# Rotary products in an attention kernel: the cosine product taken out of PSUM by VectorE, the sine product and the sum on GpSimd, and the second key and query projections ahead of the second value product

## The reference

```python
q = proj(Wq, bq) * scale            # 16 heads x 128, scale = 128 ** -0.5
k = proj(Wk, bk)
v = proj(Wv, bv)
q = t * cos(pos) + rotate_half(t) * sin(pos)     # the same for k
sim = einsum('bhid,bhjd->bhij', q, k)            # causal
out = softmax(sim) @ v
return out @ Wo + bo
```

## Time and profile before

| what | value |
|---|---|
| median of 3 runs | 1030.65 us (1030.63 to 1032.5) |
| the profiled execution's own time | 1031.39 us |
| its span, first to last instruction | 1029.6 us |
| PE busy | 970.8 us, 94% |
| DVE busy | 784.1 us, 76% |
| POOL busy | 764.7 us, 74% |
| ACT busy | 669.5 us, 65% |
| mean granted clock of TensorE | 0.996 of full |

### The profile page before, as it was taken

How to read it: one execution, slowest core, us unless ns; L and a number is a source line. 1 busy time by engine, 2 the same in 40 slices (tenths; PEclk the granted TensorE clock), 3 DMA queues, 4 the chain that set the end, 5 groups by cost and what they waited for, 6 DMA issues and landing times.

```text
span 1029.6 us, 19698 instructions
## 1 busy us (share of the span) xinstructions
PE 970.8 (94%) x5853; PEld 854.3 (83%) x5853; DVE 784.1 (76%) x1605; ACT 669.5 (65%) x1385; POOL 764.7 (74%) x532
## 2 busy tenths in 40 slices
PE   6988999999999999999999999999999999998897
PEld 5877888888888888888888888888888788887787
...
GB/s 248 166 79 139 118 118 101 107 131 114 102 101 139 127 113 111 138 127 100 115 97 141 103 111 97 148 127 107 107 142 124 109 99 159 139 103 42 1 42 42
DMA packets 86597, 116.74 MB, mean 113 GB/s; under 512 B 10468, under 2 KB 61732, under 8 KB 86564
## 3 DMA queue, kind: packets, MB, share of 16 engines
...
...
## 4 chain that ended last, share of the span: by engine, by line
PE 62%; POOL 11%; issue 7%; DMA 7%; ACT 6%; DVE 4%; SPq 2%; ACTq 0%; POOLq 0%; DVEq 0%
PE ps_r L1504 13%; PE ps_r L1503 13%; PE ps_r L1502 13%; PE ps_s L1502 5%; PE ps_s L1504 4%; PE ps_s L1503 4%; PE ps_t L1663 4%; POOL swapped L734 3%; DMA swapped<-straight 3%; POOL qk_lo L744 3%; POOL straight L735 2%; DMA side_out<-squares 2%; DMA side_p<-side_out 2%; ACT straight L885 2%; ACT probs L1014 1%
## 5 line engine op out<-in xcount | busy, mean ns | idle before, releaser
L734 POOL TENSOR_TENSOR swapped<-swapped,sin_sb 128x512 f32<-128x512 f32 x124 | 167.5, 1351 | 135.5 <-DMA swapped<-straight 135.0
L1014 ACT ACTIVATE probs<-ps_s,neg_max 128x128 f32<-128x128 f32 (+7 forms) x256 | 190.2, 743 | 109.3 <-DVE neg_max L1394 109.3
L1394 DVE CUSTOM_DVE_ANT_0 ps_s<-ps_s,mask_wide 128x128 f32<-128x128 f32 (+7 forms) x256 | 193.4, 755 | 31.1 <-PE ps_s L1504 29.4
L744 POOL TENSOR_TENSOR qk_lo<-straight,qk_hi 128x512 fp32r<-128x512 f32 x124 | 161.8, 1315 | 63.3 <-ACT qk_hi L898 63.2
L1314 DVE TENSOR_TENSOR pT_lo<-ps_t,pT_hi 128x512 fp32r<-128x512 f32 (+3 forms) x260 | 126.7, 498 | 75.7 <-ACT pT_hi L992 75.6
L735 POOL TENSOR_TENSOR straight<-straight,cos_sb 128x512 f32<-128x512 f32 x124 | 181.8, 1466 | 0.0
L1235 DVE TENSOR_TENSOR straight<-straight,swapped 128x512 f32<-128x512 f32 x126 | 147.1, 1168 | 15.2 <-POOL straight L735 14.7
L754 POOL TENSOR_TENSOR pT_lo<-side_p,pT_hi 128x1024 fp32r<-128x1024 f32 (+1 forms) x62 | 150.9, 2434 | 0.0
L1502 PE MATMUL ps_s<-qk_hi 128*128 128x512 f32 (+4 forms) x384 | 139.8, 364 | 9.7 <-POOL qk_lo L744 9.5
L992 ACT ACTIVATE pT_hi<-ps_t 128x512 fp32r<-128x512 f32 (+3 forms) x260 | 117.1, 450 | 43.0 <-PE ps_t L1663 41.3
L1353 DVE SCALAR_TENSOR_TENSOR y<-ps_r,inv_sum,y 128x256 f32<-128x256 f32 x248 | 108.4, 479 | 35.7 <-PE ps_r L1504 31.7
...
## 6 DMA issues: line engine op xcount, KB each, us to landing
...
side_p<-side_out SPq DMA_DIRECT2D x124, 128.0 KB, 3.0
...
side_p<-side_out SPq DMA_DIRECT2D x124, 112.0 KB, 2.5
...
```

The lines of the kernel that those rows point to most:

```text
L734: pool.tensor_tensor(swapped[:, q, :], swapped[:, q, :], sin_sb[:, cs], ALU.mult)
L744: pool.tensor_tensor(lo, rope_buffers(piece)[0][:, RANK[piece] % 2, :], hi.bitcast(F32), ALU.subtract)\
L1014: nc.scalar.activation(halved(t, probs[:, P_AT[step] * P:(P_AT[step] + t + 1) * P]), score_rows(step, t), ACT.Exp, bias=neg_max[:, t:t + 1 ...
L1394: nc.vector.tensor_tensor_reduce(rows, rows, halved(t, mask_wide[:, SEQ - n_keys:SEQ]), -1.0, -MASKED, ALU.add, ALU.min, accum_out=neg_max ...
```

## The change

The cosine product no longer waits for the swap. VectorE reads the projection in PSUM, adds the bias and multiplies by the cosines in one instruction (`qk_cosine`, line 1267 of the new file), into `qk_cos`, which lies where `qk_lo` of that piece will lie. GpSimd multiplies `swapped` by the sines and adds `qk_cos` to it in place. ScalarE and GpSimd then split `swapped`, not `straight`. Since the instruction has room for one scale only, the query weights are scaled as they are split (`w_high`), and the low part of the query weights moves from GpSimd to VectorE (`wq_low`, once ahead of the first units and once in a pass). TensorE's bank is now free when `cos_ready` says so. SyncE's swap now waits until the low part of the piece two before has been taken.

The plans of all engines are rewritten. On TensorE K1 goes ahead of `scores:3`, Q1 ahead of `scores:4`, and P1 behind `scores:4`.

```diff
-TENSOR_PLAN make:K0+ make:Q0+ scores:0 turn:6.0- turn:7.0- scores:1 scores:2 turn:7.1- make:P0- turn:0.0
-        make:P1- scores:3 make:W00- make:K1+ scores:4 make:W01- turn:2.0 make:Q1+
-        make:W10- scores:5 make:W11- make:V0 turn:4.0 scores:6 make:V1 turn:5.0 scores:7
-        turn:5.1
+TENSOR_PLAN make:K0+ make:Q0+ scores:0 turn:6.0- turn:7.0- scores:1 scores:2 turn:7.1- make:P0- turn:0.0
+        make:K1+ scores:3 make:Q1+ scores:4 make:P1- make:W00- turn:2.0 scores:5 make:W01- make:W10- turn:4.0
+        scores:6 make:W11- make:V0 turn:5.0 scores:7 make:V1 turn:5.1
...
-SYNC_PLAN = """swap:K0+ swap:Q0+ side:1 back:1 swap:K1+ swap:Q1+ side:3 back:3"""
+SYNC_PLAN = """swap:K0+ swap:Q0+ side:1 swap:K1+ swap:Q1+ back:1 side:3 back:3"""
...
                 sp.wait_ge(straight_ready, ps.rank(piece, 1))
+                if RANK[piece] >= 6:
+                    sp.nop(nofuse=True)
+                    sp.wait_ge(qk_ready, ps.rank(piece, -1))
...
-                pool.tensor_tensor(swapped[:, q, :], swapped[:, q, :], sin_sb[:, cs], ALU.mult)
-                pool.tensor_tensor(straight[:, q, :], straight[:, q, :], cos_sb[:, cs], ALU.mult).then_inc(rotated, 1)
+                pool.tensor_tensor(swapped[:, q, :], swapped[:, q, :], sin_sb[:, at_], ALU.mult).then_inc(rotated, 1)
+                pool.wait_ge(cos_ready, ps.cosines(piece))
+                pool.wait_ge(rotated, ps.rank(piece, 1))
+                pool.tensor_tensor(swapped[:, q, :], swapped[:, q, :], qk_cos[:, unit % 2, which, at_], ALU.add).then_inc(qk_sum, 1)
...
-                nc.scalar.activation(hi, raw, ACT.Copy).then_inc(w_hi_ready[j], 1)
+                nc.scalar.activation(hi, raw, ACT.Copy, scale=SCALE if j == WQ else 1.0).then_inc(w_hi_ready[j], 1)
...
+            def wq_low(n):
+                raw, hi, lo = w_buffers[WQ]
+                dve.wait_ge(w_hi_ready[WQ], n + 1)
+                nc.vector.scalar_tensor_tensor(lo, raw, SCALE, hi.bitcast(F32), ALU.mult, ALU.subtract).then_inc(w_ready[WQ], 1)
...
+            def qk_cosine(ps, piece):
+                dve.wait_ge(straight_ready, ps.rank(piece, 1))
+                nc.vector.scalar_tensor_tensor(qk_cos[:, unit % 2, which, at_], ps_r[:, ps.bank(piece), :], bias, cos_sb[:, at_],
+                                               ALU.add, ALU.mult).then_inc(cos_ready, 1)
...
                 if old[0] == "qk":
-                    pe.wait_ge(straight_ready, ps.rank(old, 1))
+                    if old in FIRST_QK:
+                        pe.wait_ge(straight_ready, ps.rank(old, 1))
+                    else:
+                        pe.wait_ge(cos_ready, ps.cosines(old))
```

More of the change, by code:

```diff
@@ L124 @@
     SCALAR_PLAN: """exp:0 out:K0+ xout:4 xout:5 exp:1 out:Q0+ xout:6 xout:7 exp:2 turn:0.0 exp:3 high:K0+ high:Q0+
-        side:1 exp:4 out:K1+ turn:2.0 out:Q1+ exp:5 turn:4.0 high:V0 high:V1 high:K1+ turn:5.0 exp:6 split:O side:3 turn:5.1 high:Q1+""",
-    VECTOR_PLAN: """max:0 max:1 xlow:4 xlow:5 max:2 side:1 max:3 add:K0+ xlow:6 xlow:7 turn:0.0 sum:B0 add:Q0+ sum:B1
-        max:4 gates:0 turn:2.0 side:3 max:5
-        turn:4.0 max:6 low:V0 add:K1+ low:V1 max:7 turn:5.0 add:Q1+ turn:5.1""",
@@ L129 @@
-    POOL_PLAN: """rotate:K0+ rotate:Q0+ low:K0+ low:Q0+ rotate:K1+ rotate:Q1+ low:K1+ side:1 low:Q1+ side:3 bias:0 split:O"""}
+        exp:4 out:K1+ turn:2.0 out:Q1+ side:1 exp:5 turn:4.0 high:V0 high:V1 high:K1+ turn:5.0 exp:6 split:O side:3 turn:5.1 high:Q1+""",
+    VECTOR_PLAN: """max:0 cos:K0+ max:1 xlow:4 cos:Q0+ xlow:5 max:2 side:1 max:3 xlow:6 xlow:7 turn:0.0 sum:B0 sum:B1
+        max:4 gates:0 cos:K1+ turn:2.0 side:3 max:5 cos:Q1+
+        turn:4.0 max:6 low:V0 low:V1 max:7 turn:5.0 turn:5.1""",
@@ L132 @@
+    POOL_PLAN: """rotate:K0+ rotate:Q0+ low:K0+ low:Q0+ rotate:K1+ rotate:Q1+ low:K1+ low:Q1+ side:1 side:3 bias:0 split:O"""}
 PLANS_30 = {
     TENSOR_PLAN: """make:K0+ make:Q0+ scores:0 turn:6.0- turn:7.0- scores:1 scores:2 turn:7.1- make:P0- turn:0.0
-        make:P1- scores:3 make:W00- make:K1+ scores:4 make:W01- turn:2.0 make:Q1+
-        make:W10- scores:5 make:W11- make:L0 make:L1 turn:4.0 scores:6 make:L2 make:L3 turn:5.0 scores:7
-        make:L4 turn:5.1 make:L5""",
-    SCALAR_PLAN: """out:K0+ exp:7- turn:6.0- exp:0 out:Q0+ turn:7.0- turn:7.1- float:3 high:P0- turn:0.0 exp:1 exp:2
-        high:P1- high:K0+ high:Q0+ exp:3 out:K1+ turn:2.0 exp:4 out:Q1+
-        side:1 exp:5 out:L0 turn:4.0 out:L1 high:K1+ out:L2 turn:5.0 out:L3 exp:6 side:3 turn:5.1 out:L4 high:Q1+ out:L5""",
@@ L140 @@
-    VECTOR_PLAN: """largest:0 max:0 turn:6.0- turn:7.0- turn:7.1- max:1 low:P0- add:K0+ max:2 side:1 turn:0.0 add:Q0+ largest:1
-        low:P1- max:3 sum:W00- max:4 sum:W01- turn:2.0 sum:W10- side:3 max:5 sum:W11- add:K1+
-        turn:4.0 max:6 largest:2 add:Q1+ max:7 turn:5.0 turn:5.1"""}
+        make:K1+ scores:3 make:Q1+ scores:4 make:P1- make:W00- turn:2.0 scores:5 make:W01- make:W10- turn:4.0 make:L0 make:W11-
+        make:L1 scores:6 make:L2 make:L3 turn:5.0 scores:7 make:L4 turn:5.1 make:L5""",
@@ new lines @@
+    SCALAR_PLAN: """out:K0+ exp:7- out:Q0+ turn:6.0- exp:0 turn:7.0- turn:7.1- float:3 exp:1 exp:2 high:P0- turn:0.0
+        high:K0+ out:K1+ high:Q0+ out:Q1+ exp:3 exp:4 high:K1+ high:P1- turn:2.0 high:Q1+
+        side:1 exp:5 turn:4.0 out:L0 out:L1 out:L2 turn:5.0 out:L3 exp:6 side:3 turn:5.1 out:L4 out:L5""",
+    VECTOR_PLAN: """cos:K0+ cos:Q0+ largest:0 max:0 turn:6.0- max:1 turn:7.0- max:2 turn:7.1- low:P0- side:1 turn:0.0 cos:K1+ max:3
+        cos:Q1+ max:4 side:3 low:P1- sum:W00- turn:2.0 max:5 sum:W01- sum:W10- largest:1 turn:4.0 max:6 sum:W11- largest:2 max:7
+        turn:5.0 turn:5.1"""}
@@ L1454, in do @@
                     gate_columns()
+                elif what == "split":
+                    wq_low(ps.passes(piece))
                 else:
-                    {"qk": qk_add, "v": v_low, "pv": o_low, "wo": wo_add, "bias": bias_row}[piece[0]](ps, piece)
+                    {"qk": qk_cosine, "v": v_low, "pv": o_low, "wo": wo_add, "bias": bias_row}[piece[0]](ps, piece)
             def run(ps):
```

60 lines of the change are left out of this document (37 added, 23 removed).

## The result

The changed kernel takes 1132.52 us (median of 4 runs, 1128.27 to 1133.39) against 1030.64 for the kernel before on the same chip: ratio **1.0978** [1.0946, 1.1009], 9.8% slower. The forecast was 1047.5, at most 1058. The direction was right, the size was six times too small.

What follows compares the result with a forecast made beforehand. TensorE bounds the old kernel; a new tail wait at Q0 makes units 15.81 + 12.38 = 28.2 us. 1031.4 + 14 (loop) + 2 (unit 0) + 0.7 (`wq_low`) = 1048.1 profiled, 1047.5 us median; range 1038 to 1057.

Steps and rivals of the forecast that it cites:

- ScalarE's `high:P1`: First term of the tail, behind P1's end: ScalarE's split of P1 and handover to VectorE, 0.83 us.
- VectorE without a break: Tail term after `high:P1`: VectorE working from `low:P1` to `max:6` without idling, 6.79 us with accumulator read and handover.
- 15.81: First part of a unit, TensorE from Q0's start to the end of P1, taken from the old order, in us.
- the 1.1 for the splits: Two weight splits on the tail once a pass, about 0.6 us on VectorE and 0.53 on ScalarE.
- the longer half of the unit for their way: K1 and Q1, made early, have time for swap, products and splits, so their low-part wait goes.
- the tail: Stretch from the end of P1's slot to the next unit's Q0, through ScalarE and VectorE: 12.38 us.
- The waits for `v_lo` and `y`: New TensorE waits each unit: near 0.8 us at Q0 for `v_lo`, some 0.3 each at W11 and V0 for `y`.
- Unit 0: At the start, the side tile comes 5 us late once, much of it absorbed: +2 us, between 0 and 5.
- holds, with 0.25 to spare: First half of the unit: `exp:0` takes about 2.4 us under about 2.65 of cover, so no new wait.
- rival 3: Cosine product meets GpSimd at 1.17 us or more; decided above 0.87; +17, near 1062 us; chance 0.10.
- wait of PE for `qk_lo`: TensorE's wait for the late low part of keys and queries, 9.5 us in 7 waits before, goes.
- Rival 1: Tail below 11.9 us, so the kernel gets faster: 1025 or down to 1009, middle 1018; chance 0.28.

Runs made afterwards that it cites:

- e1: Changed kernel, with VectorE waiting before the second side tile's squares only until the first was written to DRAM, not landed back: 1094.69 us, ratio 1.0612.
- e5: e1 with `high:P1` and `turn:2.0` moved ahead of `high:K1` on ScalarE in units 1 to 30: 1074.51 us, ratio 1.0420.
- e14: Changed kernel with VectorE's loop body cut from 333 to 306 instructions, its order and landed-tile wait kept: 1126.93 us, ratio 1.0915.
- e17: e14 without the eight nops of unit 0, so VectorE's loop runs from instruction 138 to 443: 1122.5 us, ratio 1.0882.
- e13: The "open tail and ends" kernel with VectorE's loop body cut from 333 to 306 instructions: 1028.52 us, ratio 0.9978.
- e15: e13 without the nops of unit 0 ahead of the loop, so VectorE's loop runs from instruction 138 to 443: 1017.82 us, ratio 0.9861.
- e9: The "tail and unit 0" kernel with `max:0` between VectorE's two cosine products, not behind both: 1047.89 us, ratio 1.0156.
- the mended order: Changed kernel's arithmetic with its waits and engine plans repaired through "open tail and ends"; e13 and e15 have it: 1028.52 and 1017.82 us.
- tail and unit 0: e5 with the tail's `turn:5.0`, `max:7` and splits reordered, query split earlier, and SyncE's old order in unit 0: 1049.67 us, ratio 1.0172.
- open tail and ends: e9 with ScalarE's side copy behind `high:V1`, VectorE's `low:V0` ahead of `turn:5.0`, and GpSimd's unit 0 and unit 30 reordered: 1030.15 us, ratio 0.9987.

## Why the prediction was wrong

- **"ScalarE's `high:P1`: 0.20 until its input is complete, 0.60, 0.03 to VectorE", in all 0.83, is the term that failed**, and with it the start of "VectorE without a break". In the unit shown, `low:P1` starts 2.99 us behind P1's end (624.32 less 621.33) and not 0.83. This is nearly the whole loss of a unit: from Q0 to P1's end it takes 16.12 us for 15.81, from there to the next Q0 14.94 for 12.66, the 12.38 and a quarter of the 1.1 for the splits (means of units 2 to 28).
- **Why it failed.** The prediction says "I checked the first half for new waits. The closest is the one at `scores:2`". It names no wait of VectorE's own there. `side:3` had moved from behind W10 to ahead of `low:P1`, and `back:1` behind the swaps; the transpose's wait for a landed tile, not seen before, holds VectorE up for 4.7 us and for 7.4 in unit 0. e1 prices it: 38 us. And ScalarE's plan has `high:K1` ahead of `high:P1`, which waits for GpSimd. e5 prices this, with the first wait gone: 20 us. The prediction gives K1 and Q1 "the longer half of the unit for their way"; there was no slack in it for what stands behind `high:K1`.
- **The rest of the tail was right, to 0.3 us.** Where only these two are mended (e5), the unit is 29.17 against 28.2 and a quarter of the 1.1 for the splits, 28.5. Of the 0.7 between, 0.3 lie from Q0 to P1's end (16.11) and 0.4 from there to the next Q0 (13.06 for 12.66): a unit without splits has 12.66 there for 12.38, and the one with the query split 0.85 more, where 0.6 was taken. The instruction itself takes 1.51 us in the changed kernel (at 627.18), in its bound of 1.8. The late start of a pass is worth 0.34 a unit from e14 to e17 and 0.43 from e13 to e15; how much of it lies in e5's 0.7 was not taken apart. The waits for `v_lo` and `y` that the forecast named are there (29.3 and 9.2 us in e5, and in the changed kernel 21.0 and 10.8), and so is VectorE's idle time ahead of the `pT_lo` of 128x512 (0.64 us in e5, for "some 0.7").
- **Unit 0 was mis-sized**: +2, between 0 and 5, where units 0 and 1 lost 14.0. The copy of the side tile waited as forecast, until 62.91 for "at 62"; what was missed is VectorE's wait beside it, and that the delay reaches the cosine product that TensorE waits for, 7.02 us in unit 0 and 4.08 in unit 1, and doesn't fall into a wait that was there.
- **`scores:2` "holds, with 0.25 to spare"** was wrong by some 0.4 us: in the changed kernel PE waits there for `exp:0` in every unit of the loop, 0.08 to 0.44 us, 0.19 on average. Taking the wait away in e9, with the tail still closed, gained 1.8 us, which is inside the noise.
- **Right**: the product is steady at 0.75 us (729 to 752 ns), so rival 3's condition never came about (its own sum, 1047.5 and 17, gives 1064.5 and not "near 1062"); no wait of PE for `qk_lo` is left among the larger ones. On the spread of the old sum the trace of the kernel before shows this: the 29 rotary sums with no GpSimd instruction beside them take 0.66 to 0.69 us, the 97 others 0.67 to 1.82, median 1.35; the new product takes 0.75 with one beside it (68) and without (56). GpSimd's sine product, the same instruction in both kernels, fell from 1351 to 1290 ns; in the kernel before the 61 that a rotary sum overlaps take 1398 ns on average, the other 63 take 1305, and in the changed kernel no such sum is beside any of them. No run took that cause alone. The first matmul behind a wait is slower, as the prediction has it: of 128x512 ones in the projections it is 0.34 us to the next one's start (19 in the kernel before), for 0.23 (median of 237).
- **What no rival had**: the place of VectorE's loop in its program, at which instruction packets come in every pass. In the mended order it is 10.7 us (e13 to e15); within the change it is about 10 with the shorter loop included (e17).
- **Rival 1, the gain**, needed a tail under 11.9 us. The mended order shows that it was there to be had (its middle was 1018, e15 has 1017.8), but not in the order as changed.

By steps, each from the run before: missed wait 37.8, `high:P1` 20.2, tail and unit 0 24.8, `max:0` 1.8, open tail and ends 17.7, shorter loop 1.6, packets 10.7: 114.7 us, from 1132.5 to 1017.8. The steps of 1.8 and 1.6 are inside the noise. So may be e14's 5.6 us: its runs spread over 8.7, and its profiled unit (31.03) is no shorter than the changed kernel's.
